# A non-local block's last stage: g and the projection as one weight, the last tile's transposes first

## The chip, the cores and the metric

One core of one Trainium2 chip runs the kernel. The metric is the device time of one execution in microseconds (us). The profile describes one execution; its span runs from the first to the last instruction that it recorded.

## The reference, cut to what matters

Four attention layers run one after the other on 32 batches of 64 x 256 float32. The first three (attention with LayerNorm and MLP, a gated one with masks, a third one with its MLP) are untouched. The change is in the last one, a non-local block over x_this (the result so far) and x_other (the context):

```python
g_x = einsum('oc,bct->bto', Wg, x_this) + bg              # Wg is 32 x 64
theta = einsum('oc,bct->bot', Wtheta, x_this) + btheta
phi = einsum('oc,bct->bot', Wphi, x_other) + bphi
f_div_C = softmax(einsum('bci,bcj->bij', phi, theta), -1)  # 256 x 256 for each batch
y = einsum('bij,bjo->bio', f_div_C, g_x)
w_y = einsum('oc,btc->bot', Wz, y) + bz                    # Wz is 64 x 32
mean, var = over batches and positions, for each of the 64 channels
return gamma * (w_y - mean) * rsqrt(var + EPS) + beta + x_this
```

Since each row of f_div_C sums to one, Wz (y) can be taken as f_div_C times (Wz Wg x_this), with the bias Wz bg + bz added once.

## The kernel before

The 32 batches make 16 tiles of 128 partitions: two batches (a = 0, 1) of 64 channels, 256 positions. Everything is resident in SBUF; `x_sb[:, t, :]` is a tile of x_this, `cx` of the context. There is one program for each engine, written out by hand, and semaphores count finished steps. Each engine's queue runs in order; a wait in it holds up all that stands behind it.

TensorE, loop `pe_tiles` over t from 0 to 17, with u = t-1 and t-2 for the later steps of older tiles:

- `pe_f` (F, L1904): scores of tile t, four matmuls with 32 contracted rows each, into two of the three banks 5 to 7. F(0) is run inside the last chunk of the last MLP.
- `pe_y` (y, L1941): four matmuls for tile t-2, each with 32 output partitions, probabilities `fT` (transposed) against the values `gx`, into bank BY.
- `pe_columns` (col, L1892): theta and phi of two tiles, at odd t.
- `pe_turn` (turn, L1930): eight 128x128 transposes of the softmax of tile t-1 into two banks BZ.
- `pe_gx` (gx, L1914): values of tile t, two matmuls of 64 columns, into the other half of BY.
- `pe_wy` (wy, L1951): projection of tile t-2, one matmul, into bank BW.

A float32 matmul shows as two records in the trace (a transpose as one).

ScalarE, `act_tiles`: copies y of t-2 to `yT` (L1974), four exps of tile t (L1982), then copies the transposes of t-1 to `fT` (L1990; the last tile in two halves, L1994). VectorE, `dve_tiles`: minimum (L2023), reciprocals of the sums (L2030), columns with their biases (L2017, L2018), values plus bg (L2049), projection plus bz (L2053), `bn_stats` (L2055). GpSimd scales the exps by the reciprocals (L2010); VectorE does that for the last tile (L2034). When all tiles are done, the statistics of the two batches of a tile are swapped between the partition halves (L2059, L2060), aggregated (L2063), and x is scaled, shifted and stored in nine pieces.

The last MLP has chunks of 512 tokens with eight steps f; step f is an "up" block W1 and a "down" block W2 of split matmuls (L175), with gelu on ScalarE (L1114, L1117) and the split on VectorE (L1085) between. `tail2` hangs the first steps of the last stage behind W2 blocks of the last chunk.

Of the kernel before, what the change touches and what calls it, by code (L numbers as in the profile page):

```python
# [49 lines left out]
for _name, _n in (("ln1", 4), ("ln2", 4), ("lnm", 4), ("l1q", 2), ("l1k", 2), ("l1v", 2), ("rms", 4), ("l2n", 4),  # L50
                  ("l2q", 2), ("l2k", 2), ("l2v", 2), ("l2m", 4), ("fb0", FT), ("fb1", FT), ("fb2", FT),
                  ("one", 4), ("bth", 1), ("bph", 1), ("bz", 1), ("gam", 1), ("bet", 1),
                  ("hmask", HPT), ("even", 1), ("odd", 1),
                  ("wth", 2 * CI), ("wph", 2 * CI), ("wg", 2 * CI), ("wz", P), ("ident", P)):
    _col(_name, _n)
# [4 lines left out]
ROWS = ("bo1", "bo2", "b_fc2", "out_b", "mlp_b2", "cproj_b", "proj_b", "bg")  # L60
# [26 lines left out]
def build(nc, wpack, ctxT, ctx_tok, x_in, mask1, mask2, cols_in, rows_in, vb_in, out, spill):  # L87
    ctx = ExitStack()
    with ctx:
# [58 lines left out]
        def row(name):  # L148
            return rows[:, ROWS.index(name), :]

# [1686 lines left out]
        def fetch_residual(e):  # L1837
# [9 lines left out]
        (F_done, pj_done, gx_done, zT_done, Y_done, wy_done, z_exp, fT_ok, yT_ok, z_min, tp_ok, gx_ok, z_rec, wy_ok, z_st, z_nrm, z_last,  # L1847
         z_c, z_pow, z_mean, z_w, z_o) = (semaphore(f"z_{n}") for n in
            "F columns g probsT Y wy exp fT yT min thetaphi gx rec wbias stats norm normlast consts pow mean scaled out".split())
        s_ct = [semaphore(f"s_ct{b}") for b in range(2)]  # L1850
        NCX = 8
        got = carve(arena, [4 * D] + [D] * NCX + [D] * 4 + [2 * 2 * CI] * 4 + [4 * D] * 2 + [D] * 2 + [TILES * D])
# [4 lines left out]
        yT, wy = got[6:8], cut(got[8], TILES)  # L1857
# [4 lines left out]
        BY, BW, BZ, BC = 0, 1, (2, 3), 4  # L1862
        LAST = TILES - 1
        PIECES = (1, 1, 2, 2, 2, 2, 2, 2, 2)

        def score_bank(t, a):


            return 5 + (2 * t + a) % 3

# [24 lines left out]
        def pe_f(e, t):  # L1895
            e.wait_ge(tp_ok, t // 2 + 1)
            if t == 0:
                e.wait_ge(mlp2["res"].sem, mlp2["res"].at(NCH - 2))
            else:
                e.wait_ge(z_exp, 2 * t - 1)  # L1900
            for ih in range(2):
                for a in range(2):
                    r = t % 2 * 2 * CI + a * CI
                    ins = e.matmul(ps[:, score_bank(t, a), ih * D:(ih + 1) * D], ph[t // 2 % 2][r:r + CI, ih * P:(ih + 1) * P],  # L1904
                                   th[t // 2 % 2][r:r + CI, :], start=True, stop=True)
            ins.then_inc(F_done, 1)

        def pe_gx(e, t):
            if t == 0:
                e.wait_ge(mlp2["gel"].sem, mlp2["gel"].at(NCH * FT - 1))  # L1910
            wait(e, yT_ok, t - 1)
            wait(e, gx_ok, t)
            for q in range(2):
                ins = e.matmul(ps[:, BY, D + q * 2 * CI:D + (q + 1) * 2 * CI], x_sb[:, t, q * P:(q + 1) * P],  # L1914
                               col("wg", 0, 2 * CI), start=True, stop=True)
            ins.then_inc(gx_done, 1)

        def pe_turn(e, u):
            if u == 0:
                e.wait_ge(mlp2["res"].sem, mlp2["res"].at(NCH - 1))  # L1920
            wait(e, fT_ok, u)
            for a in range(2):
                if u < LAST:
                    e.wait_ge(z_nrm, 2 * u + a + 1)
                else:
                    e.wait_ge(z_last, a + 1)
                for jh in range(2):
                    for ih in range(2):
                        at = (2 * jh + ih) * P
                        ins = e.transpose(ps[:, BZ[a], at:at + P], ff[u % 2][:, 2 * a + ih, jh * P:(jh + 1) * P], ident)  # L1930
                if a == 1 or u == LAST:
                    ins.then_inc(zT_done, 1)

        def pe_y(e, u):

            e.wait_ge(gx_ok, min(u + 2, TILES))
            for a in range(2):
                e.wait_ge(fT_ok, u + 1 + (a if u == LAST else 0))
                for jh in range(2):
                    to = slice((2 * jh + a) * CI, (2 * jh + a + 1) * CI)  # L1940
                    ins = e.matmul(ps[to, BY, 0:D], gx[u % 4][:, jh, a * CI:(a + 1) * CI],  # L1941
                                   fT[:, (2 * a + jh) * D:(2 * a + jh + 1) * D], start=True, stop=True)
            ins.then_inc(Y_done, 1)

        def pe_wy(e, u):

            e.wait_ge(yT_ok, u + 1)
            if u == 0:
                e.wait_ge(mlp2["gel"].sem, mlp2["gel"].at(NCH * FT - 1))
            wait(e, wy_ok, u)  # L1950
            e.matmul(ps[:, BW, 0:D], col("wz", 0, P), yT[u % 2], start=True, stop=True).then_inc(wy_done, 1)  # L1951

        def pe_tiles(e):
            for t in range(TILES + 2):
                if 1 <= t < TILES:
                    pe_f(e, t)
                if t >= 2:
                    pe_y(e, t - 2)
                if t % 2 and t + 1 < TILES:
                    pe_columns(e, (t + 1) // 2)  # L1960
                if 1 <= t <= TILES:
                    pe_turn(e, t - 1)
                if t < TILES:
                    pe_gx(e, t)
                if t >= 2:
                    pe_wy(e, t - 2)

        def act_tiles(e):
            for t in range(TILES + 2):
                u = t - 2  # L1970
                if u >= 0:
                    e.wait_ge(Y_done, u + 1)
                    wait(e, wy_done, u - 1)
                    e.activation(yT[u % 2], ps[:, BY, 0:D], ACT.Copy).then_inc(yT_ok, 1)  # L1974
# [11 lines left out]
                if 0 <= u < TILES:  # L1986
                    e.wait_ge(zT_done, u + 1)
                    wait(e, Y_done, u)
                    if u < LAST:
                        e.activation(cut(fT, 2), ps[:, BZ[0]:BZ[0] + 2, :], ACT.Copy).then_inc(fT_ok, 1)  # L1990
                    else:
                        for a in range(2):
                            e.wait_ge(zT_done, u + 1 + a)
                            e.activation(fT[:, a * 2 * D:(a + 1) * 2 * D], ps[:, BZ[a], :], ACT.Copy).then_inc(fT_ok, 1)  # L1994
# [40 lines left out]

        def dve_tiles(e):
            lower, upper = slice(0, SEQ), slice(SEQ, P)
            for t in range(TILES + 2):
                if 1 <= t < TILES:
                    dve_min(e, t)  # L2040
                if t < TILES:
                    dve_recip(e, t, 0)
                if t % 2 and t + 1 < TILES:
                    dve_columns(e, (t + 1) // 2)
                if t < TILES:
                    dve_recip(e, t, 1)
                    e.wait_ge(gx_done, t + 1)
                    wait(e, Y_done, t - 3)
                    e.tensor_tensor(gx[t % 4], cut(ps[:, BY, D:D + 4 * CI], 2), each(row("bg")[:, 0:2 * CI], 2), ALU.add).then_inc(gx_ok, 1)  # L2049
                u = t - 2  # L2050
                if u >= 0:
                    e.wait_ge(wy_done, u + 1)
                    e.tensor_scalar(wy[:, u, :], ps[:, BW, 0:D], col("bz"), None, ALU.add).then_inc(wy_ok, 1)  # L2053
                    e.wait_ge(wy_ok, u + 1)
                    e.bn_stats(bst[:, u, :], wy[:, u, :]).then_inc(z_st, 1)  # L2055
                    if u >= LAST - 1:
                        new = slice(0, LAST) if u < LAST else slice(LAST, TILES)
                        e.wait_ge(z_st, u + 1)
                        e.tensor_copy(bst[lower, TILES + new.start:TILES + new.stop, :], bst[upper, new, :])  # L2059
                        ins = e.tensor_copy(bst[upper, TILES + new.start:TILES + new.stop, :], bst[lower, new, :])  # L2060
                        ins.then_inc(z_c, 1)
# [30 lines left out]
        tail2.update({1: Parts(lambda e: pe_columns(e, 0), nothing, nothing, None), 3: Parts(nothing, nothing, lambda e: dve_columns(e, 0), None),  # L2092
                      4: Parts(lambda e: pe_f(e, 0), nothing, nothing, None), 6: Parts(nothing, nothing, lambda e: dve_min(e, 0), None)})
# [157 lines left out]
```

## Time and profile before

| | |
|---|---|
| Median of 3 runs | 1572.77 us (1572.63 to 1574.01) |
| The profiled execution | 1572.07 us, span 1570.5 us |
| TensorE matmul, weight load | 1526.3 us (97%), 1348.1 us (86%) |
| VectorE, ScalarE, GpSimd | 970.8, 857.8, 404.0 us busy |
| Granted TensorE clock, mean | 0.997 |
| DMA | 46.14 MB, mean 29 GB/s |

Engines: PE is TensorE's matmuls, PEld its weight loads, DVE VectorE, ACT ScalarE, POOL GpSimd. Busy time is an average over four very different layers; the last stage is the final 83 us of the span, and what a change in it is worth is read there. Matmuls overlap, so their durations can't be added; the distance from start to start is what a step costs.

### The profile page before, as it was taken

To read this page: it belongs to the slowest core of one execution; us is meant where nothing else is said; L and a number is where in the kernel's file an instruction comes from. 1 tells how busy PE (TensorE), PEld (TensorE's weight loads), DVE (VectorE), ACT (ScalarE), POOL (GpSimd) and SP (SyncE) were. 2 spreads that over 40 slices of the span, in tenths; PEclk is the share of its full clock that TensorE was granted. 3 is DMA by queue.
4 is the path that set the end of the run, shared out by engine and by line. 5 is a ranking of instruction groups with operands and counts; after the bars stand their busy time and mean duration, and the time that the engine had idled before them with its cause. 6 is when DMAs were issued, how large, how long until landed. Compare 5 with 4: busy or idle time off the path is not lost. (4 is left out here: it accounts for less than half of the span.)

```text
span 1570.5 us, 43145 instructions
## 1 busy us (share of the span) xinstructions
PE 1526.3 (97%) x18156; PEld 1348.1 (86%) x18156; DVE 970.8 (62%) x1999; ACT 857.8 (55%) x1624; POOL 404.0 (26%) x422
## 2 busy tenths in 40 slices
PE   8999999999999999999999999999999999999995
PEld 7888899888898998889988888988878888888863
DVE  7755555555587455555555676389996567864366
ACT  5544444444455444444444466677776567765475
POOL 1211011011124101101101214046763216531042
PEclk9999999999999999999999999999999999999998
DMA  6111011011011011100100000020002000000001
GB/s 208 36 35 35 2 36 35 2 35 35 2 36 35 2 35 36 35 2 35 35 2 29 29 14 16 1 83 2 28 3 82 1 28 3 29 2 28 12 17 54
DMA packets 18702, 46.14 MB, mean 29 GB/s; under 512 B 1456, under 2 KB 11712, under 8 KB 15440
## 3 DMA queue, kind: packets, MB, share of 16 engines
q1 hardware_dynamic: 14320, 39.17, 7.4%
q10 hardware_dynamic: 4192, 4.24, 0.8%
q8 instruction: 144, 2.36, 0.6%
q14 instruction: 46, 0.38, 0.1%
HBM read 39.21 MB, written 4.19 MB: 28 GB/s over the span
## 5 line engine op out<-in xcount | busy, mean ns | idle before, releaser
L175 PE MATMUL ps<-ch,W 128*128 128x512 f32 (+1 forms) x2592 | 597.9, 377 | 4.1 <-DVE W L243 2.3
L175 PEld LDWEIGHTS ps<-ch,W 128*128 128x128 f32 x2592 | 440.0, 188 | 85.8 <-DVE W L243 2.7
L175 PEld LDWEIGHTS ps<-W,split_arena 128*128 128x128 f32 x3084 | 392.1, 188 | 25.2 <-DVE split_arena L1085 5.0
L175 PE MATMUL ps<-W,split_arena 128*128 128x256 f32 x3084 | 406.3, 283 | 4.0 <-DVE split_arena L1085 3.2
L175 PE MATMUL ps<-W,ch 128*128 128x256 f32 x1632 | 223.1, 286 | 0.5
L175 PEld LDWEIGHTS ps<-W,ch 128*128 128x128 f32 x1632 | 203.1, 190 | 1.6 <-ACT arena L1553 1.3
L779 ACT ACTIVATE arena<-ps 64x256 f32<-64x256 f32 x256 | 96.9, 378 | 193.9 <-PE ps L692 190.8
L870 DVE TENSOR_REDUCE small<-ps 128x4 f32<-128x260 f32 x128 | 54.1, 423 | 209.7 <-PE ps L654 209.7
L210 POOL TENSOR_TENSOR arena<-arena 128x256 f32<-128x256 f32 x16 | 11.8, 739 | 586.8 <-PE ps L175 585.4
L830 ACT ACTIVATE arena<-ps,hbias 128x512 f32<-128x512 f32 x128 | 88.0, 688 | 121.0 <-PE ps L175 120.3
L955 DVE TENSOR_TENSOR arena<-ps,arena 128x512 f32<-128x512 f32 x128 | 87.9, 691 | 106.4 <-PE ps L175 106.1
L1085 DVE TENSOR_TENSOR split_arena<-arena,split_arena 128x512 fp32r<-128x512 f32 x96 | 71.5, 745 | 128.1 <-ACT split_arena L1117 118.4
L1817 POOL TENSOR_TENSOR arena<-arena,small 128x1024 f32<-128x1024 f32 x48 | 94.9, 1979 | 132.1 <-DVE small L1680 132.1
L802 ACT ACTIVATE arena<-arena 128x260 f32<-128x260 f32 x128 | 54.4, 425 | 135.8 <-DVE arena L873 135.8
L1114 ACT ACTIVATE arena<-ps,cols 128x512 f32<-128x512 f32 x96 | 65.9, 687 | 95.0 <-PE ps L175 94.9
L863 DVE SCALAR_TENSOR_TENSOR split_arena<-ps,hbias,split_arena 128x256 fp32r<-128x256 f32 x256 | 105.6, 475 | 0.0
L893 DVE TENSOR_TENSOR x_sb<-ps,x_sb 128x512 f32<-128x512 f32 x128 | 87.8, 687 | 18.7 <-PE ps L175 18.6
L786 ACT ACTIVATE split_arena<-ps,hbias 128x512 fp32r<-128x512 f32 x128 | 80.9, 683 | 27.3 <-PE ps L705 27.3
L705 PEld LDWEIGHTS ps<-arena 64*64 64x64 f32 x4096 | 65.5, 134 | 22.3 <-issue 21.8
L813 ACT ACTIVATE arena<-ps,hbias 128x512 f32<-128x512 f32 x128 | 80.0, 676 | 2.8 <-PE ps L175 2.8
L228 POOL TENSOR_TENSOR W<-raw,W 128x512 fp32r<-128x512 f32 x60 | 75.5, 1289 | 1.2
L705 PE MATMUL ps<-arena 64*64 64x64 f32 x4096 | 74.3, 221 | 0.0
(146 smaller groups left out, 1906.1 us busy)
## 6 DMA issues: line engine op xcount, KB each, us to landing
raw<-wpack SPq DMA_DIRECT2D x23, 1028.0 KB, 4.9
arena<-vb_in SPq DMA_DIRECT2D x16, 256.0 KB, 5.1
x_sb<-x_in SPq DMA_DIRECT2D x4, 512.0 KB, 8.6
arena<-ctxT SPq DMA_DIRECT2D x4, 512.0 KB, 9.4
spill<-x_sb ACTq DMA_DIRECT2D x1, 2048.0 KB, 11.0
arena<-spill ACTq DMA_DIRECT2D x1, 2048.0 KB, 9.6
arena<-ctx_tok SPq DMA_DIRECT2D x16, 128.0 KB, 2.1
out<-x_sb SPq DMA_DIRECT2D x7, 256.0 KB, 2.5
```

The source lines that it names most:

```text
L175: last = e.matmul(dst, lhs[a], rhs[b], start=start and n == 0, stop=stop and n == 2, skip_group_check=True)
L228: ins = e.tensor_tensor(W[b][1][:, a], raw[:, a], W[b][0][:, a].bitcast(F32), ALU.subtract)
L705: ins = e.matmul(ps[dims, BO + b, at:at + SEQ], vs[t % 2][keys, n, h * DH0 + d * SEQ:h * DH0 + (d + 1) * SEQ], pts[h][keys, n, :], start=T ...
L779: ins = e.activation(pts[h][b * SEQ:(b + 1) * SEQ], own[:, :, b * SEQ:(b + 1) * SEQ], ACT.Copy)
L786: e.activation(head_split(h, 0), head_cells(h), ACT.Identity, bias=head_col(t, 3, h)).then_inc(a_oh, 1)
L813: e.activation(ks[h][:, :, key_slots(h)], cut(ps[:, h, :], BPC), ACT.Identity, bias=head_col(u, 1, h)).then_inc(a_ke, 1)
L830: e.activation(qs[h], ps[:, 2 + h, :], ACT.Identity, bias=head_col(u, 0, h)).then_inc(a_qe, 1)
L863: ins = e.scalar_tensor_tensor(head_split(h, 1)[:, :, b, :], head_cells(h)[:, :, b, :], head_col(t, 3, h), head_split(h, 0)[:, :, b, :].bi ...
L893: e.tensor_tensor(xs, cut(ps[:, banks[j], :], 2), xs, ALU.add).then_inc(a_acc, 1)
L955: e.tensor_tensor(vs[u % 2][:, 2 * j:2 * j + 2, :], cut(ps[:, j, :], 2), each(vdiff[u // NCH % 2], 2), ALU.add).then_inc(a_ve, 1)
L1085: e.tensor_tensor(gsp[f % 2][1], gelu[:, f % 2, :], gsp[f % 2][0].bitcast(F32), ALU.subtract).then_inc(s["gl"].sem, 1)
L1817: e.tensor_tensor(cells, cells, many(inv[w % 2], nk), ALU.mult).then_inc(nrm_done, 1)
```

## The change

- The two weights Wz and Wg are multiplied once (`pe_merge`, `dve_merge`, two small matmuls and two VectorE instructions in step 0 of the last MLP chunk), and so are the biases. `wy` and the copy of y are gone. gx now makes 64 channels for each batch: two matmuls of 128 columns into a bank BG of its own; y is four matmuls with 64 output partitions that accumulate in pairs, and its result is the projection itself.
- The copy of gx moves from VectorE (with bg) to ScalarE (plain), at the head of ScalarE's iteration.
- TensorE's order in an iteration is F, gx, col, y, turn; it was F, y, col, turn, gx, wy.
- The last tile's transposes go ahead of y(14), into two banks that are free then, and their copy into a buffer `fT_last`.
- VectorE adds the bias of tile t-2 between or behind the reciprocals (`dve_result`), in the last three iterations ahead of them. The statistics of 14 tiles are swapped first, those of the last two at the end.
- F(0) moves from step 4 to step 6 of the last MLP chunk, its minimum from 6 to 7.

```diff
+        def pe_merge(e):
+            for at, n, x in ((0, P, col("wz", 0, P)), (P, 1, col("bgc"))):
+                lhs = col("wg", 0, P) if n == P else col("wz", 0, P)
+                ins = e.matmul(ps[:, BM, at:at + n], lhs[0:2 * CI, :], x[0:2 * CI, :], start=True, stop=True)
+            ins.then_inc(wm_done, 1)
+
+        def dve_merge(e):
+            e.wait_ge(wm_done, 1)
+            e.tensor_copy(merged, ps[:, BM, 0:P])
+            e.tensor_tensor(zbias, ps[:, BM, P:P + 1], col("bz"), ALU.add).then_inc(wm_ok, 1)
...
         def pe_gx(e, t):
-            wait(e, yT_ok, t - 1)
             wait(e, gx_ok, t)
             for q in range(2):
-                ins = e.matmul(ps[:, BY, D + q * 2 * CI:D + (q + 1) * 2 * CI], x_sb[:, t, q * P:(q + 1) * P],
-                               col("wg", 0, 2 * CI), start=True, stop=True)
+                ins = e.matmul(ps[:, BG, q * P:(q + 1) * P], x_sb[:, t, q * P:(q + 1) * P], merged, start=True, stop=True)
             ins.then_inc(gx_done, 1)
...
         def pe_turn(e, u):
-            wait(e, fT_ok, u)
+            if u < LAST:
+                wait(e, fT_ok, u)
+            else:
+                e.wait_ge(z_exp, 2 * LAST)
+                e.wait_ge(tp_ok, TILES // 2)
+            banks = BZ if u < LAST else BL
...
         def pe_y(e, u):
-            e.wait_ge(gx_ok, min(u + 2, TILES))
-            for a in range(2):
+            e.wait_ge(gx_ok, u + 1)
+            wait(e, wy_ok, u)
+            order = [(a, jh) for a in range(2) for jh in range(2)]
+            for a, jh in order if u == LAST else sorted(order, key=lambda x: x[1]):
                 e.wait_ge(fT_ok, u + 1 + (a if u == LAST else 0))
-                for jh in range(2):
-                    to = slice((2 * jh + a) * CI, (2 * jh + a + 1) * CI)
-                    ins = e.matmul(ps[to, BY, 0:D], gx[u % 4][:, jh, a * CI:(a + 1) * CI],
-                                   fT[:, (2 * a + jh) * D:(2 * a + jh + 1) * D], start=True, stop=True)
+                to = slice(a * 2 * CI, (a + 1) * 2 * CI)
+                ins = e.matmul(ps[to, BY, 0:D], gx[u % 4][:, jh, to],
+                               (fT if u < LAST else fT_last)[:, (2 * a + jh) * D:(2 * a + jh + 1) * D],
+                               start=jh == 0, stop=jh == 1, skip_group_check=True)
             ins.then_inc(Y_done, 1)
...
         def pe_tiles(e):
             for t in range(TILES + 2):
                 if 1 <= t < TILES:
                     pe_f(e, t)
+                if t < TILES:
+                    pe_gx(e, t)
+                if t % 2 and t + 1 < TILES:
+                    pe_columns(e, (t + 1) // 2)
+                if t == TILES:
+                    pe_turn(e, LAST)
                 if t >= 2:
                     pe_y(e, t - 2)
-                if t % 2 and t + 1 < TILES:
-                    pe_columns(e, (t + 1) // 2)
-                if 1 <= t <= TILES:
+                if 1 <= t < TILES:
                     pe_turn(e, t - 1)
-                if t < TILES:
-                    pe_gx(e, t)
-                if t >= 2:
-                    pe_wy(e, t - 2)
 
         def act_tiles(e):
             for t in range(TILES + 2):
-                u = t - 2
-                if u >= 0:
-                    e.wait_ge(Y_done, u + 1)
-                    wait(e, wy_done, u - 1)
-                    e.activation(yT[u % 2], ps[:, BY, 0:D], ACT.Copy).then_inc(yT_ok, 1)
+                if 1 <= t <= TILES:
+                    e.wait_ge(gx_done, t)
+                    wait(e, Y_done, t - 4)
+                    e.activation(gx[(t - 1) % 4], cut(ps[:, BG, 0:2 * P], 2), ACT.Copy).then_inc(gx_ok, 1)
...
+        def dve_result(e, u):
+            e.wait_ge(Y_done, u + 1)
+            e.tensor_scalar(wy[:, u, :], ps[:, BY, 0:D], zbias, None, ALU.add).then_inc(wy_ok, 1)
...
         def dve_tiles(e):
             for t in range(TILES + 2):
+                u, cols_too = t - 2, t % 2 and t + 1 < TILES
                 if 1 <= t < TILES:
                     dve_min(e, t)
+                if t == TILES:
+                    dve_swap(e, 0, LAST - 1)
+                if t >= LAST:
+                    dve_result(e, u)
                 if t < TILES:
                     dve_recip(e, t, 0)
-                if t % 2 and t + 1 < TILES:
+                if cols_too:
                     dve_columns(e, (t + 1) // 2)
+                elif 0 <= u and t < LAST:
+                    dve_result(e, u)
                 if t < TILES:
                     dve_recip(e, t, 1)
-                    e.wait_ge(gx_done, t + 1)
-                    wait(e, Y_done, t - 3)
-                    e.tensor_tensor(gx[t % 4], cut(ps[:, BY, D:D + 4 * CI], 2), each(row("bg")[:, 0:2 * CI], 2), ALU.add).then_inc(gx_ok, 1)
...
-        tail2.update({1: Parts(lambda e: pe_columns(e, 0), nothing, nothing, None), 3: Parts(nothing, nothing, lambda e: dve_columns(e, 0), None),
-                      4: Parts(lambda e: pe_f(e, 0), nothing, nothing, None), 6: Parts(nothing, nothing, lambda e: dve_min(e, 0), None)})
+        tail2.update({0: Parts(pe_merge, nothing, dve_merge, None), 1: Parts(lambda e: pe_columns(e, 0), nothing, nothing, None), 3: Parts(nothing, nothing, lambda e: dve_columns(e, 0), None),
+                      6: Parts(lambda e: pe_f(e, 0), nothing, nothing, None), 7: Parts(nothing, nothing, lambda e: dve_min(e, 0), None)})
```

## Rows read from the trace of the kernel before

**Rows 1.** Windows: stretch and its length, busy us (instructions) of each engine, granted clock, DMA.

```profile
1487.60:1548.90 61.30, 58.59 (x487) 38.41 (x487) 43.71 (x115) 44.01 (x143) 30.55 (x30) 1.00 0.05 14
1548.90:1558.00 9.10, 5.74 (x45) 3.43 (x42) 6.04 (x17) 4.97 (x14) 0.00 (x0) 1.00 0.00 0
1558.00:1570.50 12.50, 0.00 (x0) 0.00 (x0) 7.43 (x16) 5.81 (x10) 0.56 (x1) 0.56 0.50 168
```

**Rows 2.** Chain that ended last, one pair of tiles: start us, us, what.

```profile
1536.50 0.17 ACT arena L1974
...
1538.71 0.92 ACT arena L1990
...
1545.02 0.17 ACT arena L1974
```

**Rows 3.** Timeline of TensorE in that pair: start us, us from first start to last end.

```profile
1538.27 1.13 PE L1904 MATMUL ps<-arena 32*128 32x256 f32 x8
...
1539.76 0.64 PE L1941 MATMUL ps<-arena 128*32 128x256 f32 x8 [0.36 <-ACT arena L1990]
...
1540.33 0.65 PE L1892 MATMUL ps<-x_sb,cols 128*64 128x256 f32 x4
...
1541.35 1.10 PE L1930 MATMUL ps<-cols,arena 128*128 128x128 f32 x8
...
1542.28 0.56 PE L1914 MATMUL ps<-cols,x_sb 128*128 128x64 f32 x4
...
1542.67 0.65 PE L1951 MATMUL ps<-arena,cols 128*128 128x256 f32 x2
...
1543.25 1.13 PE L1904 MATMUL ps<-arena 32*128 32x256 f32 x8
...
1544.32 0.64 PE L1941 MATMUL ps<-arena 128*32 128x256 f32 x8
```

**Rows 4.** Waits from 1490 to 1550 us: who for whom, us, times, longest.

```profile
PEld ps L1930 <- issue: 6.0, 15, 0.4
```

**Rows 5.** Timeline of the end of the MLP and the first tiles.

```profile
1478.06 1.13 PE L1904 MATMUL ps<-arena 32*128 32x256 f32 x8
...
1485.78 1.70 PE L175 MATMUL ps<-W,split_arena 128*128 128x256 f32 x12 [0.73 <-DVE split_arena L1085]
1486.31 0.47 ACT L1982 ACTIVATE arena<-ps,small 128x256 f32<-128x256 f32 x1
...
1488.18 1.13 PE L1904 MATMUL ps<-arena 32*128 32x256 f32 x8
...
1490.09 0.47 ACT L1982 ACTIVATE arena<-ps,small 128x256 f32<-128x256 f32 x1 [1.84 <-DVE small L2023]
...
1493.77 1.10 PE L1930 MATMUL ps<-cols,arena 128*128 128x128 f32 x8
```

**Rows 6.** Timeline from the transposes of tile 14 to the aggregation.

```profile
1548.85 1.09 PE L1930 MATMUL ps<-cols,arena 128*128 128x128 f32 x8
...
1550.31 0.17 DVE L2030 RECIPROCAL small<-small 128x2 f32<-128x2 f32 x1 [0.64 <-ACT arena L1982]
...
1551.42 0.69 DVE L2034 TENSOR_TENSOR arena<-arena,small 128x512 f32<-128x512 f32 x1
...
1552.93 1.10 PE L1930 MATMUL ps<-cols,arena 128*128 128x128 f32 x8
...
1553.71 1.09 ACT L1994 ACTIVATE arena<-ps 128x512 f32<-128x512 f32 x2 [0.26 <-PE ps L1930]
...
1555.52 0.38 ACT L1974 ACTIVATE arena<-ps 128x256 f32<-128x256 f32 x1 [0.72 <-PE ps L1941]
...
1555.96 0.70 PE L1951 MATMUL ps<-arena,cols 128*128 128x256 f32 x2 [0.48 <-ACT arena L1974]
1556.69 0.48 DVE L2053 TENSOR_SCALAR arena<-ps,cols 128x256 f32<-128x256 f32 x1 [0.80 <-PE ps L1951]
...
1558.05 1.02 DVE L2063 BATCH_NORM_AGGREGATE small<-norm_arena 128x2 f32<-128x192 f32 x1
```

More of the change, by code:

```diff
@@ L58 @@
 PJB = (0, 1, 2, 3)
[L60 removed]
+ROWS = ("bo1", "bo2", "b_fc2", "out_b", "mlp_b2", "cproj_b", "proj_b")
 class Steps:
@@ L1845, in build @@
         next2.lead, next2.after_act = mlp2_start, nothing
-        (F_done, pj_done, gx_done, zT_done, Y_done, wy_done, z_exp, fT_ok, yT_ok, z_min, tp_ok, gx_ok, z_rec, wy_ok, z_st, z_nrm, z_last,
+        (F_done, pj_done, wm_done, gx_done, zT_done, Y_done, z_exp, fT_ok, wm_ok, z_min, tp_ok, gx_ok, z_rec, wy_ok, z_st, z_nrm, z_last,
          z_c, z_pow, z_mean, z_w, z_o) = (semaphore(f"z_{n}") for n in
-            "F columns g probsT Y wy exp fT yT min thetaphi gx rec wbias stats norm normlast consts pow mean scaled out".split())
+            "F columns merged g probsT Y exp fT mergedout min thetaphi gx rec wbias stats norm normlast consts pow mean scaled out".split())
         s_ct = [semaphore(f"s_ct{b}") for b in range(2)]
         NCX = 8
-        got = carve(arena, [4 * D] + [D] * NCX + [D] * 4 + [2 * 2 * CI] * 4 + [4 * D] * 2 + [D] * 2 + [TILES * D])
+        got = carve(arena, [4 * D] + [D] * NCX + [D] * 4 + [D] * 4 + [4 * D] * 2 + [P + 1] + [TILES * D] + [4 * D])
         fT, cx, th, ph = got[0], got[1:1 + NCX], got[1 + NCX:3 + NCX], got[3 + NCX:5 + NCX]
@@ L1856, in build @@
         ff = [cut(g, 4) for g in got[4:6]]
-        yT, wy = got[6:8], cut(got[8], TILES)
+        merged, zbias, wy, fT_last = got[6][:, 0:P], got[6][:, P:P + 1], cut(got[7], TILES), got[8]
         bst = cut(norm_arena[:, 0:2 * TILES * 6], 2 * TILES)
@@ L1986, in act_tiles @@
                 if 0 <= u < TILES:
-                    e.wait_ge(zT_done, u + 1)
-                    wait(e, Y_done, u)
                     if u < LAST:
+                        e.wait_ge(zT_done, u + 1)
+                        wait(e, Y_done, u)
                         e.activation(cut(fT, 2), ps[:, BZ[0]:BZ[0] + 2, :], ACT.Copy).then_inc(fT_ok, 1)
@@ L2034, in dve_recip, with dve_swap @@
                 e.tensor_tensor(part, part, many(zrec[t % 2][:, half], D), ALU.mult).then_inc(z_last, 1)
+        def dve_result(e, u):
+            e.wait_ge(Y_done, u + 1)
+            e.tensor_scalar(wy[:, u, :], ps[:, BY, 0:D], zbias, None, ALU.add).then_inc(wy_ok, 1)
+        def dve_swap(e, first, last):
+            lower, upper = slice(0, SEQ), slice(SEQ, P)
+            e.wait_ge(z_st, last)
+            e.tensor_copy(bst[lower, TILES + first:TILES + last, :], bst[upper, first:last, :])
+            e.tensor_copy(bst[upper, TILES + first:TILES + last, :], bst[lower, first:last, :]).then_inc(z_c, 1)
@@ L2051, in dve_tiles @@
                 if u >= 0:
-                    e.wait_ge(wy_done, u + 1)
-                    e.tensor_scalar(wy[:, u, :], ps[:, BW, 0:D], col("bz"), None, ALU.add).then_inc(wy_ok, 1)
                     e.wait_ge(wy_ok, u + 1)
                     e.bn_stats(bst[:, u, :], wy[:, u, :]).then_inc(z_st, 1)
[L2056 to L2061, printed above, removed]
+            dve_swap(e, LAST - 1, TILES)
```

34 lines of the change are left out of this document (15 added, 19 removed).

## The prediction

> **What bounds the kernel now.** I read the stages first, then the chain that ended last, then the timeline of one pair of tiles, and last the beginning and the end of the stage. [rows 1] cut the end of the span into the tile loop (61.3 us), its last tile (9.1 us) and the output (12.5 us). The reader is to see that TensorE is busy 58.59 of 61.3 us in the loop at full clock, but does nothing in the output, where the granted clock falls to the lower level; no matmul stands there, so the clock costs nothing. The change touches only the loop, its last tile, and one insertion into the MLP ahead. I name the steps by the tile: F(t) scores, gx(t), col the columns for two tiles, turn(t) the transposes, y(t).
>
> [rows 2] give the period: the copy of y for every second tile starts at 1536.50 and at 1545.02, so a pair costs 8.52 us. [rows 3] show this pair on TensorE. Start to start: y 0.57, col 1.02, turn 0.93, gx 0.39, wy 0.58, F 1.07. Two of each and one col make 8.10 us; the other 0.42 is the stop before y at 1539.76 (F started 1.49 us, not 1.07, ahead of it), which waits for ScalarE's copy fT. So half of the pair is bound by TensorE, half by the round y, copy of y, exps, fT, y.
>
> **The change, part by part.** All prices are start to start, because matmuls overlap.
>
> *wy and the copy of y go*: 2 x 0.58 = 1.16 us less on TensorE in a pair; ScalarE's 0.38 us copy of y is replaced by a copy of gx with the same shape.
>
> *y is wider.* Four matmuls still stream 256 columns, but each takes 64 columns of the array instead of 32, so two run side by side, not four. No row shows that shape at work on y; col has exactly its form (four matmuls, 128x64 tiles, 256 columns) and costs 1.02. Bounds are 0.57 (as before) and 1.06 (F, also in pairs); I take 1.02, so +0.90 in a pair. Where y follows col directly the tile size doesn't change; I take 0.86 for col there.
>
> *gx is wider*: 128 columns instead of 64, four records. The turn's eight records of 128 columns take 0.93, so 0.12 each; four make 0.47, and a change of tile size behind them adds what it adds elsewhere, some 0.11: 0.58. Bounds are 0.39 (the old row) and 0.71 (as the last third of the range of such changes, 0.24, would give).
>
> *Tile sizes.* gx now stands between F (32x128) and y (128x64). [rows 4] show what a change costs the weight loads: 15 waits of 0.4 us for no semaphore ahead of the turn. Part is hidden behind matmuls in flight; it is inside the start-to-start prices. The Trainium skill (TensorEngine Tiling (Array Packing), Tiling Modes) says that changing the tiling mode drains TensorE; by that rule the new order has eight changes in a pair where the old has seven, which speaks against the change. By the rows the extra one is the 0.11 in gx, some 0.2 in a pair.
>
> A dense TensorE would so cost: even tile F 1.07 + gx 0.58 + y 1.02 + turn 1.05 (0.93 and a change) = 3.72; odd 0.86 more; pair 8.30, against 8.52 now. But it can't be dense:
>
> *The new wait.* gx(t) writes the one bank BG and waits for gx_ok, the copy of gx(t-1). That copy opens ScalarE's iteration t, so it is queued behind fT(t-2), which ends iteration t-1 and waits for turn(t-2), TensorE's last step of iteration t-1. Behind the waiting gx on TensorE stand col, y and the next turn. Before, DVE made this copy (0.29 us) and nothing of ScalarE stood ahead of it. The round, from the start of one turn to the next:
> - turn start to its end as ScalarE sees it: four transposes took 0.78 (1552.93 to 1553.71, [rows 6]), four more at 0.11 to 0.12 less the slower first: the eight last 1.10; so 1.11
> - fT: 0.92 on the chain [rows 2] and 0.02: 0.94 until the next ScalarE work
> - the copy of gx: 0.38, as the 128x256 copy in [rows 6], and 0.06 until TensorE starts (1555.90 to 1555.96)
> - gx 0.58, y 1.02
>
> Sum 4.09 for an even tile, 4.95 for an odd one with col. F(t), 1.05 after the turn and 1.07 long, ends inside the 2.49 us to gx. Pair 9.04: 0.52 slower than now. The wait itself is 2.49 - 1.05 - 1.07 = 0.37 us a tile. Nothing else is late in this round: exps start 1.91 after F's start (1488.18 to 1490.09, [rows 5]) and last some 1.9, so they end 4.86 after the turn's start, 0.34 before the next fT; VectorE's and GpSimd's work ends earlier still.
>
> *Head.* The merge puts two matmuls (four records) behind the first W2 block of the last MLP chunk, where TensorE is the bound. Nearest rows are gx (0.39) and col (1.02); I take 0.59, four loads and a change on either side. F(0) leaves a dense place, where it cost 1.06, for the place ahead of the last W2 block, which waited 0.73 us for VectorE's split [rows 5]. Everything up to there comes 1.06 sooner, and F(0) fills the gap and runs 0.42 over it (with a change): net 0.64 gained. With the merge: 0.05 gained, nothing. exps(0) start at F(0) + 1.91 = 1486.58 in place of 1486.31, which delays nobody: F(1) needs only their first half. So F(1) stands at 1488.15 (1488.18 before). Then gx(1) 1489.22, col 1489.80, turn(0) 1490.82, and turn(1) 4.09 later: 1494.91, against 1493.77: +1.14. Much of that is order only (the turn now stands behind gx), given back at the end.
>
> *Loop.* From turn(1) to turn(14) there are 13 rounds, six with col: 13 x 4.09 + 6 x 0.86 = 58.33 us; before 1548.85 - 1493.77 = 55.08 [rows 5, 6]: +3.25.
>
> *Last tiles, from the start of turn(14).* y(13) ends at +0.07, the VectorE result of tile 13 (0.43) now stands ahead of the reciprocal of tile 15, so reciprocal at +0.55 and the second product done 1.80 later (1550.31 to 1552.11, [rows 6]), +2.35. The second half of turn(15) at +2.40; y(14) 0.7 later, 3.1; it ends at 4.2, its result at 4.73 (y(15) waits for that, one bank). y(15) at 4.78; its four matmuls of one half share their 64 columns of the array and run one behind the other: at best like col, 1.1 us to the end, at worst eight steps of 0.22 and the drain, 2.0. I take 1.7: 6.5. From result to aggregation 1.36 (1556.69 to 1558.05): 7.89. Before: 1558.05 - 1548.85 = 9.20. So -1.31 from no wy, no copy of y, no copy of gx ahead of y(14), and the swap of 14 tiles' statistics done ahead. Behind the aggregation nothing changes (12.5 us).
>
> **Sum**: 1.14 + 3.25 - 1.31 = +3.1 us. The profiled execution had 1572.07 around its span of 1570.5, so 1575.2 in its measure; the median of the runs shown is 0.7 above it, so 1575.8 there (+0.20%). What a measurement of this kernel can tell from no change is about 0.2%, 3.15 us: the forecast lies on that line.
>
> **The rivals.**
> *The copy of gx is hidden (faster side).* If turn's end, fT and the copy take 0.37 us less a tile than I read, TensorE is dense: 13 x 3.72 + 6 x 0.86 = 53.5 in the loop (-1.6), turn(1) +0.8, end -1.3: -2.1, 1570.7. It decides at a gap of 2.12 us from turn to gx. For it: ScalarE is busy only 44.0 of 61.3 us of the loop [rows 1], so it looks free. Against: the order of its queue, and each link of 2.49 has a row. The Trainium skill (TensorEngine Tiling (Array Packing), PSUM Bottleneck) advises both ScalarE and VectorE for emptying PSUM; the change instead takes gx from VectorE and gives it to ScalarE. Followed, that advice would give this rival's time; no run here shows it yet. 12%.
>
> *The wider shapes cost more than their rows.* gx's 128-column records might run like wy's (0.29 each with the change) or the merge might stall the MLP as col did (1.02). gx at 0.86 costs 0.28 x 14 = +3.9: 1579.7; half of it 1577.8. For it: gx loads full 128x128 weights for each record. Against: the transposes load as much at 0.12. 15%.
>
> *y costs what it did* (0.57, columns in fours): 0.45 x 14 = -6.3, 1569.5. Only if col's 1.02 came from something else than its width; 3%.
>
> **How the numbers follow.** The forecast's mechanism 70%, its own range 1574.0 to 1577.4: gx from 0.50 (-1.1) to 0.66 (+1.1), end and head 0.4 each way. The remaining 30% are the rivals. Slower by over 0.2% (above 1575.9): half of the forecast's case and the whole of the dear shapes, 50%. Within 0.2%: the other half and most of the hidden copy, 45%. Faster: 5%. Range 1573.2 to 1578.2: it leaves out the two cheap cases in the main and the dearest half of the dear one.
>
> **What would show it.** In the loop: a period of 9.0 us a pair; a stop of TensorE of about 0.4 us ahead of each gx that the ScalarE copy of gx ends, that copy directly behind fT; y at about 1.0 start to start; the chain of a pair through turn, fT, copy, gx, y. At the head F(1) near 1488.2. At the end 7.9 us from turn(14) to the aggregation. The prediction is wrong if the stop isn't there (8.3 a pair), if gx takes much over 0.6, or if the head moves by more than half a us.

## Result

The changed kernel takes 1576.24 us (median of 18 runs, 1575.39 to 1579.0) where the kernel before takes 1572.73 (18 runs). The ratio is 1.0023, 95% interval 1.0017 to 1.003: slower by 3.5 us. The forecast was 1575.8, +0.20%, by a new wait ahead of gx. The profiled execution of the changed kernel took 1578.66 us with a span of 1577.1, which is 2.4 above its median, and this has a cause of its own. The first two lines are windows of the changed kernel, the third is the same window of the kernel before:

```profile
1370.00:1380.00 10.00, 8.38 (x163) 7.38 (x161) 7.48 (x14) 5.96 (x9) 8.29 (x13) 0.77 0.02 3
1380.00:1385.00 5.00, 4.39 (x86) 3.90 (x86) 3.23 (x5) 2.84 (x5) 1.16 (x2) 0.79 0.00 0
```

```profile
1370.00:1380.00 10.00, 8.28 (x233) 7.24 (x232) 8.77 (x16) 7.11 (x12) 9.03 (x14) 1.00 0.01 3
```

They stand in the third layer, far ahead of all that was changed; behind the busy times of the five engines comes the granted clock: 0.77 and 0.79 after, 1.00 before. About 6.8 us ran at the lower of its two levels, 1.2 in place of 2.4 GHz. Such a stretch, of 3.4 or 6.8 us, shows in seven of the fourteen profiled executions, the kernel before with one part changed among them. Here it costs 3.0 us: the transposes ahead of the last MLP chunk come 3.7 us later than before, and 0.7 of that is something else (experiments 9 to 11). So I don't compare spans, but distances behind that place.

### The profile page after: what moved, and what is told of

Read it like the earlier page. It is cut to its first block and busy times, and to the rows that moved or that the text cites. A ratio compares the mean times of both kernels' runs of the same rounds, so it can differ in the third digit from the quotient of the medians.

```text
span 1577.1 us, 43030 instructions
## 1 busy us (share of the span) xinstructions
PE 1532.5 (97%) x18128; PEld 1354.2 (86%) x18128; DVE 967.3 (61%) x1985; ACT 859.4 (54%) x1624; POOL 403.6 (26%) x422
## 5 line engine op out<-in xcount | busy, mean ns | idle before, releaser
L210 POOL TENSOR_TENSOR arena<-arena 128x256 f32<-128x256 f32 x16 | 11.8, 740 | 587.5 <-PE ps L175 586.0
```

## The profile after

First the loop, the timeline of a pair of tiles in the changed kernel (start, us from first start to last end; in brackets the idle time ahead and who ended it):

```profile
1544.24 1.09 PE L1948 MATMUL ps<-cols,arena 128*128 128x128 f32 x8
...
1545.27 1.13 PE L1919 MATMUL ps<-arena 32*128 32x256 f32 x8
...
1546.72 0.71 PE L1928 MATMUL ps<-arena,x_sb 128*128 128x128 f32 x4 [0.33 <-ACT arena L1985]
...
1547.37 0.65 PE L1906 MATMUL ps<-x_sb,cols 128*64 128x256 f32 x4
...
1548.28 1.03 PE L1960 MATMUL ps<-arena 128*64 128x256 f32 x8
...
1549.24 1.09 PE L1948 MATMUL ps<-cols,arena 128*128 128x128 f32 x8
...
1550.27 1.13 PE L1919 MATMUL ps<-arena 32*128 32x256 f32 x8
1550.37 1.02 ACT L2001 ACTIVATE arena<-ps 128x1024 f32<-128x1024 f32 x1 [1.19 <-PE ps L1948]
1551.29 0.38 ACT L1985 ACTIVATE arena<-ps 128x256 f32<-128x256 f32 x1
...
1551.72 0.71 PE L1928 MATMUL ps<-arena,x_sb 128*128 128x128 f32 x4 [0.33 <-ACT arena L1985]
...
1552.37 1.08 PE L1960 MATMUL ps<-arena 128*64 128x256 f32 x8
...
1553.38 1.09 PE L1948 MATMUL ps<-cols,arena 128*128 128x128 f32 x8
```

The reader is to follow one round: the turn starts at 1549.24; ScalarE idles until it ends and starts fT at 1550.37; the copy of gx stands directly behind it, 1551.29 to 1551.67; gx starts at 1551.72, with an idle TensorE ahead of it although F began at 1550.27; y 0.65 later, the next turn at 1553.38. That is 4.14 us for a tile without col and 5.00 with it (1544.24 to 1549.24), 9.14 for a pair against 8.52 in [rows 2]. (L1919 is F, L1928 gx, L1906 col, L1960 y, L1948 the turn; L2001 is fT and L1985 the copy of gx.) The view of waits from 1492 to 1558 us counts it (who for whom, us, times, longest):

```profile
PE ps L1928 <- ACT arena L1985: 4.2, 13, 0.3
```

Thirteen stops of 0.33 us ahead of gx. In the same view of the kernel before, from 1490 to 1550 us, there is no wait of gx.

Then the head and the first turns of the changed kernel, in its timeline, against [rows 5]:

```profile
1469.26 0.60 PE L1888 MATMUL ps<-cols 64*128 64x128 f32 x4
1469.79 1.66 PE L175 MATMUL ps<-ch,W 128*128 128x512 f32 x6
...
1488.16 1.13 PE L1919 MATMUL ps<-arena 32*128 32x256 f32 x8
...
1489.22 1.70 PE L175 MATMUL ps<-W,split_arena 128*128 128x256 f32 x12
...
1491.68 1.13 PE L1919 MATMUL ps<-arena 32*128 32x256 f32 x8
...
1498.54 1.09 PE L1948 MATMUL ps<-cols,arena 128*128 128x128 f32 x8
```

The merge (L1888) costs 0.53 from its start to the next block, and F(0) at 1488.16 now fills the place ahead of the last block. Last the end, against [rows 6]:

```profile
1557.52 1.09 PE L1948 MATMUL ps<-cols,arena 128*128 128x128 f32 x8
1557.64 0.48 DVE L2049 TENSOR_SCALAR arena<-ps,arena 128x256 f32<-128x256 f32 x1 [0.77 <-PE ps L1960]
...
1558.04 0.16 DVE L2041 RECIPROCAL small<-small 128x2 f32<-128x2 f32 x1
...
1559.03 0.69 DVE L2045 TENSOR_TENSOR arena<-arena,small 128x512 f32<-128x512 f32 x1
...
1560.36 1.08 PE L1960 MATMUL ps<-arena 128*64 128x256 f32 x8
1561.50 0.48 DVE L2049 TENSOR_SCALAR arena<-ps,arena 128x256 f32<-128x256 f32 x1 [0.99 <-PE ps L1960]
...
1562.08 1.09 PE L1960 MATMUL ps<-arena 128*64 128x256 f32 x8 [0.64 <-issue]
1563.22 0.48 DVE L2049 TENSOR_SCALAR arena<-ps,arena 128x256 f32<-128x256 f32 x1 [0.77 <-PE ps L1960]
...
1564.58 1.02 DVE L2082 BATCH_NORM_AGGREGATE small<-norm_arena 128x2 f32<-128x192 f32 x1
```

From turn(14) to the aggregation it takes 7.06 us, before 9.20. Two idle places of TensorE are left: 0.64 ahead of y(15), which waits until VectorE has y(14) out of the bank, and the wait for the products (L2045) ahead of the last transposes. The distances start from the transposes ahead of the last MLP chunk, here before and after the change:

```profile
1441.95 1.04 PE L546 MATMUL ps<-cols,norm_arena 128*128 128x128 f32 x8
```

```profile
1445.67 1.03 PE L546 MATMUL ps<-cols,norm_arena 128*128 128x128 f32 x8
```

All distances together, in us:

| stretch | before | after | difference | forecast |
|---|---|---|---|---|
| transposes ahead of the last MLP chunk to F(1) | 46.23 | 46.01 | -0.22 | -0.03 |
| F(1) to turn(1) | 5.59 | 6.86 | +1.27 | +1.17 |
| turn(1) to turn(14) | 55.08 | 58.98 | +3.90 | +3.25 |
| turn(14) to aggregation | 9.20 | 7.06 | -2.14 | -1.31 |
| aggregation to the end | 12.45 | 12.52 | +0.07 | 0 |
| sum | | | +2.9 | +3.1 |

The medians differ by 3.5; the missing 0.6 must stand ahead of these distances, in layers that the change doesn't touch, and three of the experiments are about it.

## The experiments

Each was timed against the kernel before in five rounds, except where it is said. Numbers for a place are distances in the trace.

**1. Is it the order of ScalarE's queue? The copy of gx ahead of fT.**

```diff
         def act_tiles(e):
             for t in range(TILES + 2):
-                if 1 <= t <= TILES:
-                    e.wait_ge(gx_done, t)
-                    wait(e, Y_done, t - 4)
-                    e.activation(gx[(t - 1) % 4], cut(ps[:, BG, 0:2 * P], 2), ACT.Copy).then_inc(gx_ok, 1)
                 if t < TILES:
...
+                if t < TILES:
+                    e.wait_ge(gx_done, t + 1)
+                    wait(e, Y_done, t - 3)
+                    e.activation(gx[t % 4], cut(ps[:, BG, 0:2 * P], 2), ACT.Copy).then_inc(gx_ok, 1)
                 u = t - 1
                 if 0 <= u < TILES:
```

> The changed kernel with one thing moved: ScalarE copies gx(t) behind the exps of tile t and ahead of fT(t-1), no longer behind fT. My theory (the loop is set by the round turn, fT, copy of gx, gx, because of the order of ScalarE's queue): the stop of 0.33 us ahead of gx goes, TensorE is dense, a pair of tiles takes 2 x (F 1.07 + gx 0.65 + y 1.01 + turn 1.03) + col 0.86 = 8.38 us instead of 9.14; over 6.5 pairs 4.9 us less than the changed kernel, about 1571.3, 0.1% under before. Rival (the wider y and gx set the time, the wait only stands beside them): the pair stays over 9 us and the time at 1576.

Measured: 1571.08 us, ratio 0.9993 (0.9984 to 1.0002); the pair takes 8.35 us. Its timeline of TensorE:

```profile
1518.04 1.13 PE L1919 MATMUL ps<-arena 32*128 32x256 f32 x8
1519.11 0.71 PE L1928 MATMUL ps<-arena,x_sb 128*128 128x128 f32 x4
1519.75 1.08 PE L1960 MATMUL ps<-arena 128*64 128x256 f32 x8
1520.76 1.09 PE L1948 MATMUL ps<-cols,arena 128*128 128x128 f32 x8
1521.79 1.13 PE L1919 MATMUL ps<-arena 32*128 32x256 f32 x8
```

gx follows F after 1.07 us with no idle time. One instruction moved in one queue takes 5.2 us off the median; turn(1) to turn(14) falls from 58.98 to 53.82, under the 55.08 before. The wait was the cause of the slower loop; with the wider shapes alone the time can't be told from that of the kernel before.

**2. Is it the engine? The copy taken off ScalarE, as in 1, and put on VectorE behind the minimum.**

```diff
                 if 1 <= t < TILES:
                     dve_min(e, t)
+                if t < TILES:
+                    e.wait_ge(gx_done, t + 1)
+                    wait(e, Y_done, t - 3)
+                    e.tensor_copy(gx[t % 4], cut(ps[:, BG, 0:2 * P], 2)).then_inc(gx_ok, 1)
```

> The changed kernel with the copy of gx(t) on VectorE behind the minimum of tile t, as the work was shared before. My theory: the same dense TensorE, a pair of 8.38 us, about 1571.3; what counts is the order and not the engine. Rival (ScalarE's load counts, so moving work off it gives more than reordering it): clearly under the run with the copy ahead of fT. Rival (the copy delays VectorE's reciprocals and with them GpSimd and the turn): over it, by up to the 0.3 us of the copy in each tile, 4 us.

Measured: 1570.62 us, ratio 0.9987 (0.9978 to 0.9996); the pair again 8.35, turn(1) to turn(14) 53.82 as in 1. The two medians lie 0.5 apart, inside their intervals, and from the last MLP on their traces agree to 0.02 us. What counts is what stands ahead of the copy in its queue, not which engine makes it. The Trainium skill (TensorEngine Tiling (Array Packing), PSUM Bottleneck) advises to use both engines for emptying PSUM. Both empty it in experiments 1 and 2 alike; for this one copy the trace shows the same 8.35 us a pair on either of them, once it stands at the right place.

**3. gx behind the turn, its place before the change.**

```diff
             for t in range(TILES + 2):
                 if 1 <= t < TILES:
                     pe_f(e, t)
-                if t < TILES:
-                    pe_gx(e, t)
...
                 if 1 <= t < TILES:
                     pe_turn(e, t - 1)
+                if t < TILES:
+                    pe_gx(e, t)
```

> The changed kernel with gx(t) behind turn(t-1) on TensorE, its place before the change; ScalarE's queue as changed. My theory: gx has the tile size of the turn, so a change of tile size goes and gx costs about 0.5; fT and the copy have F and y as cover. Even tile F 1.07 + y 1.01 + turn and gx 1.5 = 3.64, or 3.73 where exps and fT set it; pair 8.15 to 8.25; turn(1) 1.0 sooner. Together 6.9 us under the changed kernel, about 1569.4, 0.2% under before. Rival (a change of tile size costs nothing that counts): the same as with the copy ahead of fT, 1571.3.

Measured: 1568.07 us, ratio 0.9975 (0.9966 to 0.9984). Its timeline of TensorE:

```profile
1516.54 1.13 PE L1919 MATMUL ps<-arena 32*128 32x256 f32 x8
1517.61 1.08 PE L1960 MATMUL ps<-arena 128*64 128x256 f32 x8
1518.62 1.09 PE L1948 MATMUL ps<-cols,arena 128*128 128x128 f32 x8
1519.55 0.61 PE L1928 MATMUL ps<-arena,x_sb 128*128 128x128 f32 x4
1520.09 1.13 PE L1919 MATMUL ps<-arena 32*128 32x256 f32 x8
```

The pair takes 7.96 us, less than I expected: an even tile 3.55, not 3.64 to 3.73, so exps and fT set nothing here. Turn and gx together cost 1.47 us (0.93 and 0.54), in experiment 1 they cost 1.67 (1.03 and 0.64). These are the same matmuls in the same number; what differs is that gx now has a neighbour of its own tile size, which is one change of tile size less. It makes 0.2 us a tile. The view of waits fits: over the 13 rounds the weight loads stop for no semaphore for 11.8 us in experiment 1, 4.6 of them in 14 stops at gx, and for 8.0 us here, none of them at gx. That agrees with the rule of the Trainium skill that a change of tiling mode drains TensorE (TensorEngine Tiling (Array Packing), Tiling Modes). That the tile size, and nothing else about the neighbour, makes the 0.2 us was not tried by itself.

**4. VectorE's result of tile 13 behind the reciprocals of tile 15.**

```diff
-                if t >= LAST:
+                if t >= TILES:
                     dve_result(e, u)
...
-                if cols_too and u >= 0:
+                if (cols_too or t == LAST) and u >= 0:
                     dve_result(e, u)
```

> The changed kernel, with VectorE's result of tile 13 behind the reciprocals and products of tile 15 instead of ahead. My theory: the reciprocal of tile 15 waits 0.7 us for y(13) there; without it the second product ends 0.55 sooner, and so do turn(15), y(14), y(15) and the end: 1575.7 against 1576.2. Rival (y(14), which waits for that result, becomes late instead): no change, 1576.2.

Measured: 1575.85 us, ratio 1.0023 (1.0014 to 1.0032). In the trace turn(14) to aggregation falls from 7.06 to 6.58, by 0.48 where 0.55 was expected; the times alone can't tell it from the changed kernel.

**5. y(14) ahead of the last transposes.**

```diff
-                if t == TILES:
-                    pe_turn(e, LAST)
                 if t >= 2:
                     pe_y(e, t - 2)
+                if t == TILES:
+                    pe_turn(e, LAST)
```

> The changed kernel with y(14) ahead of the last tile's transposes, as the order was before the change. My theory (the transposes first are worth their place at the end, because y(14) must wait for fT(14) anyway): y(14) starts 0.05 after fT(14), 1559.7 in the changed kernel's times, the transposes 1.0 later, fT_last 0.6 later than now, so y(15) starts 0.5 to 0.6 later and the end with it: 1576.8. Rival (the bank of y(15), free only after y(14)'s result, sets the end, and that result comes sooner here): no change or a gain of up to 0.6.

Measured: 1576.8 us, ratio 1.0021 (1.0012 to 1.003); the end of its timeline:

```profile
1557.45 1.08 PE L1960 MATMUL ps<-arena 128*64 128x256 f32 x8 [1.20 <-ACT arena L2001]
...
1558.47 1.09 PE L1948 MATMUL ps<-cols,arena 128*128 128x128 f32 x8
...
1559.90 1.48 PE L1960 MATMUL ps<-arena 128*64 128x256 f32 x8 [0.34 <-ACT arena L2005]
```

TensorE stands idle for 1.20 us for the copy of fT(14), which the transposes fill in the changed kernel. Turn(14) to aggregation 7.63, 0.57 longer. This part of the change is a gain, as expected. That the bank holds up y(15) is not the limit in this order.

**6 and 7. The two parts of the head, each alone in the kernel before.** F(0) in step 6 and its minimum in step 7:

```diff
-                      4: Parts(lambda e: pe_f(e, 0), nothing, nothing, None), 6: Parts(nothing, nothing, lambda e: dve_min(e, 0), None)})
+                      6: Parts(lambda e: pe_f(e, 0), nothing, nothing, None), 7: Parts(nothing, nothing, lambda e: dve_min(e, 0), None)})
```

> The kernel before with one part of the change alone: F(0) in step 6 and its minimum in step 7 of the last MLP chunk. My theory: F(0) fills the 0.73 us in which the last W2 block waited for VectorE's split, so F(1) comes 0.75 us sooner and the end 0.7, about 1571.8; in the changed kernel the merge's 0.53 eats most of it. Rival (the minimum, now in the last step, makes the first exps late): no gain, 1572.5.

Measured: 1571.63 us, ratio 0.9984 (0.9975 to 0.9993); F(1) comes 1.01 us sooner (45.22 for 46.23). The merge alone, of the same size, with a result that isn't used, and F(0) waits for it as in the changed kernel:

```diff
+        def pe_merge(e):
+            for at, n in ((0, P), (P, 1)):
+                ins = e.matmul(ps[:, 5, at:at + n], col("wz", 0, P)[0:2 * CI, :], col("wz", 0, n)[0:2 * CI, :], start=True, stop=True)
+            ins.then_inc(wm_done, 1)
...
+        def dve_merge(e):
+            e.wait_ge(wm_done, 1)
+            e.tensor_copy(wy[:, 0, 0:P], ps[:, 5, 0:P])
+            e.tensor_tensor(wy[:, 0, P:P + 1], ps[:, 5, P:P + 1], col("bz"), ALU.add).then_inc(wm_ok, 1)
...
+        tail2.update({0: Parts(pe_merge, nothing, dve_merge, None), 1: Parts(lambda e: pe_columns(e, 0), nothing, nothing, None), 3: Parts(nothing, nothing, lambda e: dve_columns(e, 0), None),
```

> The kernel before with one part of the change alone: a merge of the same size (two matmuls over 64 rows, four records, and the two VectorE instructions; its result isn't used) in step 0 of the last MLP chunk. My theory: TensorE is the bound there and the merge takes its 0.53 us, so F(1) comes 0.53 later and the time is 1573.1. Rival (it hides in the waits of the MLP): no change in F(1)'s distance. Besides: if the 0.8 us in the attention layers comes from the length of the instruction stream, part of it can show here; if from addresses of data, none.

Measured: 1573.57 us, ratio 1.0007 (0.9998 to 1.0016); F(1) comes 0.72 later (46.95). The merge between its two blocks:

```profile
1465.97 1.59 PE L175 MATMUL ps<-W,split_arena 128*128 128x256 f32 x12
1467.50 0.60 PE L1885 MATMUL ps<-cols 64*128 64x128 f32 x4
...
1468.03 1.66 PE L175 MATMUL ps<-ch,W 128*128 128x512 f32 x6
...
1469.53 1.59 PE L175 MATMUL ps<-W,split_arena 128*128 128x256 f32 x12
```

0.53 of the 0.72 are its own place. The rest stands on its two sides: the W2 block ahead of it takes 1.53 from start to start and the W1 block behind it 1.50, where the pair just before takes 1.43 and 1.39. -1.01 and +0.72 make -0.29, the changed kernel shows -0.22: the parts nearly add up, and both were larger than I took them.

**8. y(15) in the bank of gx, on top of 3.**

```diff
...
-            wait(e, wy_ok, u)
+            if u < LAST:
+                wait(e, wy_ok, u)
+            bank = BY if u < LAST else BG
...
-                ins = e.matmul(ps[to, BY, 0:D], gx[u % 4][:, jh, to],
+                ins = e.matmul(ps[to, bank, 0:D], gx[u % 4][:, jh, to],
...
-            e.tensor_scalar(wy[:, u, :], ps[:, BY, 0:D], zbias, None, ALU.add).then_inc(wy_ok, 1)
+            e.tensor_scalar(wy[:, u, :], ps[:, BY if u < LAST else BG, 0:D], zbias, None, ALU.add).then_inc(wy_ok, 1)
```

> The kernel with gx behind the turn, and y(15) into the bank of gx, which is free by then, so that it needn't wait until VectorE has taken y(14) out of its bank. My theory (that wait, 0.63 us of TensorE idle, is on the path): y(15) starts 0.65 sooner and the end comes 0.6 sooner than with gx behind the turn alone (1568.1), 1567.4. Rival (VectorE's result and statistics of tile 14, which must come first, are next to end): at most 0.2 less.

Measured: 1567.29 us (five runs), ratio 0.9956 (0.9943 to 0.997). Its timeline:

```profile
1549.33 2.00 PE L1962 MATMUL ps<-arena 128*64 128x256 f32 x16
1550.46 0.48 DVE L2051 TENSOR_SCALAR arena<-ps,arena 128x256 f32<-128x256 f32 x1 [0.99 <-PE ps L1962]
...
1551.37 0.48 DVE L2051 TENSOR_SCALAR arena<-ps,arena 128x256 f32<-128x256 f32 x1
...
1552.74 1.02 DVE L2084 BATCH_NORM_AGGREGATE small<-norm_arena 128x2 f32<-128x192 f32 x1
```

y(14) and y(15) are one run of 16 records; from turn(14) to aggregation it is 6.44 us, in 3 it was 7.25. That is 0.81 less in the trace and 0.8 in the medians. The wait for the bank was on the path.

**9 to 12. The time lost where nothing was changed.** In the first layer, which has two attentions, the matmuls that stream 256 columns against W are a little longer in the changed kernel. These are the groups of instructions between 110 and 900 us, with busy time and mean ns, of the kernel before, the changed kernel, the padded one (9) and the one with the table kept (10):

```profile
L175 PE MATMUL ps<-W,ch 128*128 128x256 f32 x1344 | 183.4, 286 | 0.0
```

```profile
L175 PE MATMUL ps<-W,ch 128*128 128x256 f32 x1344 | 184.1, 287 | 0.0
```

```profile
L176 PE MATMUL ps<-W,ch 128*128 128x256 f32 x1344 | 184.1, 286 | 0.0
```

```profile
L176 PE MATMUL ps<-W,ch 128*128 128x256 f32 x1344 | 183.4, 286 | 0.0
```

Experiment 9 puts the large buffers back to their old addresses:

```diff
+        sb("pad", 191)
         split_arena = sb("split_arena", 4096, F32R)
```

> The changed kernel with 191 unused words ahead of the split buffer in SBUF, which puts all buffers behind the constants back to the addresses that they had before the change (the table of rows had lost 256 words, the columns had gained 65). The traces of the changed kernel and of every version of it fall behind by 0.8 us over the two attention layers at the start, which the change doesn't touch, always at the same three matmuls of a step. My theory (the new addresses of the buffers make these slower): the 0.8 goes, 1575.4. Rival (the addresses of the constants themselves or of the instructions do it, or chance): it stays, 1576.2.

Measured: 1576.07 us, ratio 1.0017 (1.0008 to 1.0026), and the group stays at 184.1. The place of the large buffers isn't it. Experiment 10 leaves the table of constants as it was and hangs the new entries on its end:

```diff
-                  ("one", 4), ("bth", 1), ("bph", 1), ("bz", 1), ("bgc", 1), ("gam", 1), ("bet", 1),
+                  ("one", 4), ("bth", 1), ("bph", 1), ("bz", 1), ("gam", 1), ("bet", 1),
...
-                  ("wth", 2 * CI), ("wph", 2 * CI), ("wg", P), ("wz", P), ("ident", P)):
+                  ("wth", 2 * CI), ("wph", 2 * CI), ("free", 2 * CI), ("wz", P), ("ident", P), ("wg", P), ("bgc", 1)):
...
+        sb("pad", 127)
```

> The changed kernel with the table of constants in its old order: the wider weight and the bias of g are appended behind the identity, 64 unused columns stand in the old place, and 127 unused words put the buffers behind back to their old addresses. The identity and all that the attention layers read so has its old address. My theory now (the operands' place in SBUF makes the three matmuls of a step slower): the 0.8 us in the first 930 us goes, 1575.4. Rival (it is the instruction stream, whose length changed): it stays, 1576.1.

Measured: 1575.72 us, ratio 1.002 (1.0011 to 1.0029), and the group is back at 183.4. The drift is gone too: between the same instructions near 110 and 930 us the changed kernel falls 0.66 us behind the kernel before, this one not at all. In the medians of 9, 10 and the changed kernel such a difference can't be told from none. Experiment 11 is a look at the kernel before once more, unedited:

> The kernel before once more, for a second trace of it: if the 0.8 us in the attention layers belongs to the change, this trace keeps step with the first one there to within 0.1 us from the first matmuls on; if it is chance, it drifts as the others do.

One time, 1572.86 us; the group again 183.4, as in experiments 6 and 7, and no drift from 110 to 930 us. The four other traces with the old table keep step with the first one there to within 0.05 us, all nine with the new table fall 0.63 to 0.67 behind. So it isn't chance, and it isn't the instruction stream, which experiment 10 leaves as it is in the changed kernel: it is where the constants lie. The identity, which the transposes of this layer read, moved from word 399 to word 464 of the table; that it is this entry and no other was only argued. The table of rows behind it moved as well (counted from the start of the first table, it begins at word 527 before, 592 after and 656 in experiment 10), and that this plays no part was not shown.

The second trace of the kernel before sets a limit to all this: its transposes ahead of the last MLP chunk come at 1442.67, 0.7 later than in the first trace, with not a word changed. Some 0.3 of that is there from the start, the rest comes between 1175 and 1250 us, as in seven of the fourteen traces. So of the 0.6 us that the medians have over the distances, the drift is a likely source (0.66 up to 930 us, of which 0.12 comes back before 1370), but not a measured one. Experiment 12 joins 8 and 9:

> The kernel with gx behind the turn and y(15) in the bank of gx, and the 191 unused words. The padding alone changed nothing (its trace shows the same 0.65 to 0.8 us in the attention layers), so the time of the version without it: 1567.3, 0.35% under before. Rival (the padding did give the 0.2 us by which its median was lower): 1567.1, which this run can't tell.

Measured: 1567.07 us (five runs), ratio 0.9963 (0.995 to 0.9977). The lowest median of all versions, 0.37% under the kernel before and 9.2 us under the changed one; from experiment 8 it can't be told. Joined with the old table it was not tried.

## Why the prediction was right

**The new wait** was foreseen with its place, its releaser and its round: turn, fT, copy of gx, gx, y. Forecast 4.09 and 4.95, measured 4.14 and 5.00. In the round the link from turn to gx was 2.49 by my sum and is 2.48 (1549.24 to 1551.72); y 1.02 and 1.01. The stop of TensorE is 0.33 where I had 0.37. Experiment 1 shows the cause by taking it away.

**gx** was a little dearer: 0.65 start to start, not 0.58. Over 13 rounds that is 0.9 us of cost, and with smaller differences in the other links the loop cost 3.90 for 3.25. In experiment 3, without the change of tile size behind the turn, the pair of turn and gx shows where it comes from.

**The end** gained more than I took, 2.14 for 1.31. The term that was mis-sized is y(15): I took 1.7 us because its matmuls stand in the queue half by half, first both of one half of the array, then both of the other, and took them to run one behind the other; it has 1.09, as long as y(14) in the alternating order, and 1.14 to its result. And y(14) starts 2.84 after turn(14), not 3.1. (By my own terms the end is 6.5 and 1.36, 7.86; the sum carried 7.89.) That the result of y(13) holds up the reciprocal by half a us was right (experiment 4), and that y(15) waits for the bank as well (experiment 8).

**The head** was taken as zero because two parts cancel: -0.64 and +0.59. They do cancel, but are -1.01 and +0.72. F(0) gave back more at its old place than the 1.06 I took: the W2 block ahead of the last one starts 40.22 after the transposes in experiment 6 and 41.50 before, 1.28 sooner. And at its new place it runs 0.26 over the gap (2.59 between the last two W2 blocks for 2.33), not 0.42.

**What I didn't see** is the place of the constants, 0.66 us by 930 us in a layer that I had taken as untouched. With the dearer gx it made up for what the end gave more. That the total came within 0.4 us is so partly luck: the end was 0.8 and the head 0.2 too dear in my sum, the loop 0.65 and the way from F(1) to turn(1) 0.1 too cheap, and 0.6 in the medians has no term in it.

**The rivals.** The hidden copy (1570.7) was wrong for this order, and is just what experiments 1 and 2 made: 1571.1 and 1570.6. The dearer shapes (gx at 0.86) and the unchanged y (0.57) are ruled out by the rows after, with gx at 0.65 and y at 1.01.

So the change in itself was good (fewer instructions on TensorE's path, a better end) and was lost to one queue order: the same edits with gx at its old place are 0.25% faster than before, not 0.23% slower.

## What to carry to other kernels

When work moves to an engine with idle time, ask what stands ahead of it in that engine's queue and whom that waits for: ScalarE was busy 72% of the loop before the change, and afterwards made TensorE wait 13 times, because the copy stood behind an instruction that waits for the last step of the tile before. Keep steps with the same tile size next to each other on TensorE; here the neighbour was worth 0.2 us a tile. And a widened table of constants moves every entry behind it, which here lengthened matmuls that don't read it; appending to its end left them as they were.

## What the runs showed of the hardware that was not expected

- Column tiles overlap although they are queued apart. y(15) queues the four records for columns 0 to 63 and then the four for 64 to 127, y(14) alternates: 1.09 and 1.08 us from first start to last end. In both the records start in pairs, a pair every 0.22 us; which half a record belongs to the trace doesn't say, but eight one behind the other at that distance would take over 1.7.
- The place of constants in SBUF changes matmuls that don't read them: 183.4 us for the same 1344 matmuls in each of the five traces with the table's old order, 184.1 in each of the nine with the new one. Which constant does it, and how, stays open.
- The granted clock fell to the lower level for 3.4 or 6.8 us, starting at 1163 us or at 1375 to 1378 us, towards the end of the attention of the second and of the third layer, in seven of the fourteen profiled executions. In the changed kernel it fell at 1375.3, 0.1 us after TensorE had taken up work again behind 1.5 us of idleness. But the kernel before is idle there for the same 1.5 us, is as busy in the same window (8.28 us of ten for 8.38), and keeps the full clock. None had it in the last stage before the matmuls ended. What decides between the two stays open.
